# Attention scores of a decoder as plain fp32 products on four groups of 32 partitions, with the maximum as a row of the queries

## The reference, cut to what matters

```python
q = _heads(x @ Wq + bq)                       # (8, 16, 512, 16)
k = _heads(x @ Wk + bk)
v = _heads(x @ Wv + bv)
att = jnp.einsum('bhqd,bhkd->bhqk', q, k) * scale
att = jnp.where(causal[None, None], att, -jnp.inf)
y = jnp.einsum('bhqk,bhkd->bhqd', jax.nn.softmax(att, axis=-1), v)
qc = _heads(x @ Wcq + bcq)
kc = _heads(cross_input @ Wck + bck)          # 1024 context positions
vc = _heads(cross_input @ Wcv + bcv)
attc = jnp.einsum('bhqd,bhkd->bhqk', qc, kc) * scale
y = y + jnp.einsum('bhqk,bhkd->bhqd', jax.nn.softmax(attc, axis=-1), vc)
```

## Time and profile before

| | |
|---|---|
| Median of the runs | 2286.91 us |
| The profiled execution | 2287.69 us, its span 2286.0 us |
| PE (matmul) busy | 2169.5 us, 95% of the span |
| DVE (VectorE) busy | 1366.7 us, 60% |
| ACT (ScalarE) busy | 1102.2 us, 48% |
| POOL (GpSimd) busy | 367.5 us, 16% |
| Mean granted TensorE clock | 0.994 |

### The profile page before, as it was taken

One profiled execution on the slowest core, in us unless ns is written; L12 is line 12 of the kernel. 1 busy time (PEld: TensorE's weight loads), 2 busy tenths in 40 slices (PEclk: granted clock), 3 DMA queues, 4 the chain that ended last, 5 costly groups with the idle time before them and its releaser, 6 DMA issues. The chain is left out here.

```text
span 2286.0 us, 51067 instructions
## 1 busy us (share of the span) xinstructions
PE 2169.5 (95%) x16290; PEld 1352.2 (59%) x16291; DVE 1366.7 (60%) x3905; ACT 1102.2 (48%) x1680; POOL 367.5 (16%) x628
## 2 busy tenths in 40 slices
PE   8999999999899999999999999999999899799998
PEld 4555554556455555555555645554555455499997
DVE  2588357844785458635883478357844685255554
ACT  1267524761477227732674257524762377233332
POOL 1011111111111111111111111111111111122222
PEclk9999999999999999999999999999999999899999
DMA  7440025102520162005300350026102520655553
GB/s 235 155 164 25 2 106 200 48 2 85 198 71 2 47 234 73 2 11 189 130 25 9 141 180 25 1 97 209 48 2 85 198 71 2 221 181 182 183 182 109
DMA packets 115763, 235.75 MB, mean 103 GB/s; under 512 B 19614, under 2 KB 42655, under 8 KB 113344
## 3 DMA queue, kind: packets, MB, share of 16 engines
q1 hardware_dynamic: 112112, 224.23, 29.3%
q0 software_dynamic: 3408, 8.41, 1.0%
HBM read 154.04 MB, written 73.17 MB: 99 GB/s over the span
## 5 line engine op out<-in xcount | busy, mean ns | idle before, releaser
L1201 ACT ACTIVATE es<-ps 128x1024 f32<-128x1024 f32 (+1 forms) x704 | 665.3, 984 | 250.7 <-PE ps L809 181.4
L1412 DVE TENSOR_REDUCE craw<-ps 128x1 f32<-128x512 f32 x1024 | 636.7, 684 | 115.0 <-PE ps L773 115.0
L773 PE MATMUL ps<-hk,hq 64*128 64x512 f32 x1024 | 391.4, 450 | 24.7 <-DVE craw L1412 8.6
L807 PE MATMUL ps<-hq,hk 64*128 64x512 f32 x1024 | 325.0, 440 | 2.2 <-ACT es L1201 2.2
L1408 DVE CUSTOM_DVE_ANT_0 ps<-ps,causal 128x512 f32<-128x512 f32 (+3 forms) x512 | 236.2, 518 | 91.4 <-PE ps L770 91.0
L773 PEld LDWEIGHTS ps<-hk,hq 64*128 64x128 f32 x1024 | 174.7, 184 | 194.8 <-DVE craw L1412 129.3
L809 PE MATMUL ps<-mrow,minus 64*128 64x512 f32 x1024 | 285.8, 391 | 0.0
L837 PE MATMUL ps<-es,vca 128*17 128x256 f32 x4096 | 276.6, 382 | 1.2 <-ACT es L1201 0.3
L661 POOL TENSOR_SCALAR_AFFINE_SELECT es<-es 128x256 f32<-128x256 f32 x256 | 99.0, 406 | 659.5 <-ACT es L1201 659.4
L1731 ACT ACTIVATE hT<-ph,b1s 128x128 f32<-128x128 f32 x312 | 89.2, 369 | 182.8 <-PE ph L1694 182.8
L809 PEld LDWEIGHTS ps<-mrow,minus 64*128 64x128 f32 x1024 | 166.0, 186 | 10.1
(11 more groups left out here) (210 smaller groups left out, 2838.3 us busy)
## 6 DMA issues: line engine op xcount, KB each, us to landing
w1s<-in_w1T SPq DMA_DIRECT2D x39, 1024.0 KB, 5.4
hk<-scr_kc SPq DMA_DIRECT2D x64, 512.0 KB, 5.1
scr_kc<-staged SPq DMA_DIRECT2D x16, 1024.0 KB, 4.3
scr_qc<-staged SPq DMA_DIRECT2D x32, 512.0 KB, 4.5
scr_q<-staged SPq DMA_DIRECT2D x32, 512.0 KB, 5.3
hq<-scr_qc SPq DMA_DIRECT2D x56, 256.0 KB, 4.4
hq<-scr_q SPq DMA_DIRECT2D x56, 256.0 KB, 4.2
hk<-scr_k SPq DMA_DIRECT2D x56, 256.0 KB, 4.6
```

Of the source, the lines that this page charges most:

```text
L773: last = mm(pb, hq[i][at, T + t * P:T + (t + 1) * P], hk[i][at, T + half * BANK:T + (half + 1) * BANK], start=True, stop=True)
L807: mm(pb[a], hk[i][rows[a], T + j * P:T + (j + 1) * P], hq[i][rows[a], T:2 * T], start=True, stop=False)
L1201: nc.scalar.activation(es[:, k % ERING, :].rearrange("p (a c) -> p a c", a=HB)[:, :, 0:w], eslot[k % 2][:].rearrange("p (a c) -> p a c", a ...
L1412: last = v.reduce_max(craw[p % 2][:, t, a:a + 1, 1 + half], pb, AX.X)
```

## The change

- **Products.** The scores are plain fp32 matmuls over 32 partitions. A head's 16 channels lie in every other one of 32 partitions (ROWS), twice: the two heads of a pair have groups 0 and 1 (partitions 0 to 63) for the exponentials and groups 2 and 3 for the maxima. No high and low parts are made.
- **The maximum.** The odd rows of `hk` hold -1, those of `hq` 0. SyncE copies a pair's turned maxima by two DMAs into one odd row of `hq` in groups 0 and 1 (`place_maxima`). The score product then subtracts the maximum itself, and the second matmul is gone. The turned maxima are 16 rows, which ScalarE copies in one instruction in place of four.
- **Staging.** ScalarE or VectorE write each projection once, with its bias, to SBUF (`stage_part`), and SyncE loads a pair's rows from there, each load twice (two DMAs). There are no stores to DRAM and no scratch. There are 4 slots in place of 5, and they are set once by GpSimd (8 memsets before the loop).
- **Order.** One step a cycle: the step k, two maxima (three in the first four steps), then the `weigh` unit of step k-3. After a pair's last `weigh` one cycle goes without, and the next has two and then the turn. Before the steps there are 27 maxima between the parts and 3 behind; the row of a pair goes four maxima behind its last one (two for the first pair).

```diff
-EARLY = 2
-ROW_AFTER = (4, 6)
-BEHIND = 4
-SLOTS = 5
+SLOTS = 4
+LEAD = SLOTS - 1
+MORE_FIRST = 4
+ROW_AFTER = 4
+FIRST_ROW = 2
+BEHIND = 3
 FIRST_PARTS = [("v", 1, 3), ("qc1", 0, 3), ("q1", 0, 3), ("k1", 0, 3),
-               ("qf0", 0, 4), ("qf0", 1, 4), ("qf1", 0, 4), ("qf1", 1, 4)]
+               ("qf0", 0, 4), ("qf0", 1, 4), ("qf1", 0, 4), ("qf1", 1, 3)]
...
-    turns, late = [], []
+    turns, held, kept = [], [], False
     steps = PAIRS * NU
-    for k in range(0, steps + BEHIND, 2):
...
+    for k in range(steps + BEHIND):
+        if k < steps:
+            order.append(("exp", *divmod(k, NU)))
+        order += take(HB + (k < MORE_FIRST))
+        if k >= BEHIND:
+            held.append(k - BEHIND)
+        if kept and k < steps:
+            kept = False
+            continue
+        for m in held:
             order.append(("weigh", *divmod(m, NU)))
             if m % NU == NU - 1:
                 order.append(("keep", m // NU, 0))
+                kept = True
                 turns.append(("turn", m // NU, 0))
...
+        if held and held[0] % NU == 0 and turns:
+            order.append(turns.pop())
+        held = []
...
+            def load(name, p, to, col, done):
+
+                of, first = stage[name], p % (PAIRS // 2) * HB * XD
+                w = of.shape[-1]
+                for u in range(2):
+                    sp.dma_start(to[p % SLOTS][u * HB * ROWS:(u + 1) * HB * ROWS:2, col:col + w],
+                                 of[first:first + HB * XD, p // (PAIRS // 2), :]).then_inc(done[p % SLOTS], 16)
...
+            def place_maxima(b, p):
+
+                sp.wait_ge(s_turned, cur(b, PAIRS, p + 1))
+                sp.sem_inc(s_pace, 1)
+                for a in range(HB):
+                    at = a * ROWS + MAXROW
+                    sp.dma_start(hq[p % SLOTS][at:at + 1, :].rearrange("p (n c) -> p n c", c=P),
+                                 mrow[p % 2][a * 2 * NT:(a + 1) * 2 * NT, :]).then_inc(s_mrow, 16)
...
+            for i in range(SLOTS):
+                nc.gpsimd.memset(hk[i][:], -1.0)
+                nc.gpsimd.memset(hq[i][:], 0.0).then_inc(s_minus, 1)
...
-                pb, at = ring_slot(b, ("max", p, m)), slice(a * HROW, (a + 1) * HROW)
+                pb, first = ring_slot(b, ("max", p, m)), (HB + a) * ROWS
+                at = slice(first, first + ROWS)
...
                 if n == 0:
-                    pe.wait_ge(s_mrow, cur(b, PAIRS, p + 1))
+                    pe.wait_ge(s_mrow, (b * PAIRS + p + 1) * HB * 16)
...
-                    for a in turned:
-                        mm(pb[a], hk[i][rows[a], T + j * P:T + (j + 1) * P], hq[i][rows[a], T:2 * T], start=True, stop=False)
-                    for a in turned:
-                        last = mm(pb[a], neg[a], mrow[p % 2][rows[a], :], start=False, stop=True)
+                rows = [slice(a * ROWS, (a + 1) * ROWS) for a in range(HB)]
+                for j, col in (EXP_SELF[n] if n < NSELF else [(n - NSELF, 0)]):
+                    key, query, w = (j * P, j * P, T - j * P) if n < NSELF else (T + j * P, T, T)
+                    for a in range(HB):
+                        last = mm(pb[a][:, col:col + w], hk[i][rows[a], key:key + P], hq[i][rows[a], query:query + w],
+                                  start=True, stop=True)
...
-                    for t in range(NT):
-                        last = nc.scalar.activation(mrow[p % 2][:, t * P:(t + 1) * P], mbank[n % MBANKS][:, 0:P],
-                                                    ACT.Copy, scale=inblock[:, t:t + 1])
+                    nc.scalar.activation(mrow[p % 2][:], mbank[n % MBANKS][0:MCOLS, 0:P], ACT.Copy).then_inc(s_turned, 1)
```

More of the change, by code:

```diff
@@ L143, in heads_order @@
     order += take(MAXES + AHEAD - sum(count for _, _, count in FIRST_PARTS))
-    turns, late = [], []
+    turns, held, kept = [], [], False
     steps = PAIRS * NU
-    for k in range(0, steps + BEHIND, 2):
[L147 to L150, removed]
-        for m in weighed:
-            if m % NU == 0 and m and order[-1] == ("keep", m // NU - 1, 0):
-                late.append(m)
-                continue
+    for k in range(steps + BEHIND):
[8 more added lines that the diff above has]
+        for m in held:
             order.append(("weigh", *divmod(m, NU)))
@@ L157, in heads_order @@
                 order.append(("keep", m // NU, 0))
+                kept = True
                 turns.append(("turn", m // NU, 0))
-        order += take(1)
-        if k < steps:
-            order.append(("exp", *divmod(k, NU)))
-        order += take(HB)
-        if k + 1 < steps:
-            order.append(("exp", *divmod(k + 1, NU)))
-        order += take(1)
-        order += [("weigh", *divmod(m, NU)) for m in late]
-        late = []
+        if held and held[0] % NU == 0 and turns:
+            order.append(turns.pop())
+        held = []
     assert not maxima
@@ L320, in attentions @@
         x1 = sb("x1", [P, NT, CR])
-        with nc.sbuf_tensor("x1T", [P, KC, T], F32) as x1T:
-            pass
-        hq.append(sb("hq4", [P, 2 * T], F32R))
-        craw = [sb(f"craw{i}", [P, NT, HB, 3]) for i in range(2)]
-        minus = sb("minus", [P, 2], F32R)
-        minus_f = sb("minus_f", [P, 2])
-        inblock = sb("inblock", [P, NT])
+        x1T = sb("x1T", [P, KC, T])
+        craw = [sb(f"craw{i}", [P, NT, HB, 2]) for i in range(2)]
         zk = sb("zk", [P, 2, T // 2])
@@ L566, in _ @@
+            sp.wait_ge(s_minus, SLOTS)
             with sp.Fori(0, nb) as b:
                 following = sp.snap((b + 1) % nb)
-                store(b, "kc0")
                 sp.wait_ge(s_xb, cur(b, 2, 1))
@@ L1140, in _, with stage_part @@
                 nc.scalar.activation(g_s[:, 0, :], t[:], ACT.Copy).then_inc(s_act, 1)
-                def high_part(name, bias_n, m, w, last=True):
-                    stg, at, before = STAGED[name]
-                    t = full(name)
-                    for n in before:
-                        act.wait_ge(s_st[n], cur(b, ST[n], 0 if n in LAST_STAGED else ST[n]))
-                    high = nc.scalar.activation(stage[:, stg, 0, at:at + w], t[:, 0:w], ACT.Identity,
-                                                bias=bias_c[:, bias_n, m:m + 1])
-                    if last:
-                        high.then_inc(s_act, 1)
+                def stage_part(name, bias_n):
+                    m = int(name[-1])
+                    of = stage[name[:-1]]
+                    nc.scalar.activation(of[:, m, :], full(name)[:, 0:of.shape[-1]], ACT.Identity,
+                                         bias=bias_c[:, bias_n, m:m + 1]).then_inc(s_act, 1)
                 t = full("g1")
                 nc.scalar.activation(g_s[:, 1, :], t[:], ACT.Copy).then_inc(s_act, 1)
-                high_part("kc0", 1, 0, TC_)
+                stage_part("kc0", 1)
                 t = full("kv")
@@ L1401, in reduce @@
                     n, a = divmod(m, HB)
+                    if (n, a) == (2 * NT, 0) and p >= 2:
+                        dve.wait_ge(s_ring, cur(b, NRING, RING_AT["row", p - 2, 0] + 1))
+                        dve.sem_inc(s_held, 1)
                     dve.wait_ge(s_ring, cur(b, NRING, s + 1))
```

269 lines of the change are left out of this document (79 added, 190 removed), and 6 rows, old and new, of the table JOBS.

## The result

| | before | after |
|---|---|---|
| Median of the runs | 2287.57 us (4 runs beside it) | 2697.06 us (4 runs, 2678.96 to 2710.71) |
| Ratio | | 1.1785, 95% interval 1.1715 to 1.1855 |
| The profiled execution, its span | 2287.69, 2286.0 us | 2697.38, 2695.7 us |
| Mean granted TensorE clock | 0.994 | 0.977 |
| Period of a sequence without time at half clock | 240.9 us | 285.9 us |

The forecast was 2641 us, range 2480 to 2790. The change costs 409 us.

A forecast was written before the change was run, and what follows sets the result against it. TensorE was taken to set the pace. Heads +37.3, last `weigh` run -0.4, before the steps +8.0 and staging -0.7 gave 44.2 us a sequence, 354 for eight; 2287.7 + 354 - 0.8 gave 2641 us, range 2480 to 2790.

The forecast's parts named there:

- The array's passes: Score products on TensorE: an fp32 pass starts every 0.43 us, four products run abreast, 0.86 us of passes a step.
- The rival by which four groups slow each other: Score products in four row groups: a pass takes 0.56 us instead of 0.43, 0.26 more a step, 2820 us; chance 9%.
- Two passes that hold up the next product: Score products start strictly in program order: five places of 0.43 us, not two, +1.29 a step, 3540 us; chance 3%.
- A step with maxima: Heads: 1.62 us of PE work plus 0.135 of waiting makes 1.755 us a step, 71 steps a sequence, 124.6 us.
- Without maxima: Last 17 steps of a sequence's heads: 1.62 us each for scores and one `weigh` unit, 27.5 us.
- The bank's wait: Three-bank ring: a step's second maximum waits 0.135 us for the bank of the first maximum one step earlier.
- The heads of a sequence: All 88 steps with rows, turns and own units: 165.0 us against 127.7, +37.3; forecast wrong under 150 or over 180.
- Before the steps: Rounds of maxima ahead of the first step: 35.2 us in place of 27.15, +8.0 a sequence, bounds +4 and +11.
- Staging and the row's DMAs at nothing: Projection staging and the maxima row's two DMAs (3.6 us in all) stay hidden; only a 0.68 us wait goes, -0.7.
- The order: Rows of maxima among the steps: seven rows a sequence at 0.6 us each, 4.2 us; the eighth was given nothing.
- The clock: TensorE's granted clock: read at full clock in every slice but one before; no term for half clock in the sum.
- the forecast's 0.11 and 0.1 around the passes: Each step's scores on PE: 0.11 us for first weights, about 0.1 to run out before the array changes shape.

The follow-up runs named there:

- half the reduction: The changed kernel with VectorE reducing only 256 of the 512 columns of each cross unit, leaving half of the cross keys out of its maxima: 2583.95 us, ratio 1.1297.

## Why the prediction was right, and where it missed

- **The array's passes**: right. Passes start 0.43 apart (L734 at 563.12, 563.55 and 563.98), in four groups abreast. The rival by which four groups slow each other is out: 1.07 us for four products, 1.06 for two, and a second pair of products costs 0.96 us in the same groups. The Trainium skill ("TensorE: Matmul & The Clock Gate", Part 3) has 3.07x for row packing of four products. No run here has the four one behind another; by an estimate of 4 x 0.86 and 0.2 around them it would be 3.64 us, 3.4 times the 1.07.
- **Two passes that hold up the next product**: out. The maxima's first passes start at 467.74, ahead of the second passes of the exponentials' products at 468.26, though those products stand ahead in the program. The same Part of the Trainium skill says that matmuls start strictly first in, first out. By products the trace agrees (467.73 and then 467.74); pass by pass, as the rival reads it, it doesn't.
- **A step with maxima**: 1.755 forecast, 1.77 and 1.80 in turn. **Without maxima**: 1.62 forecast, 1.61. **The bank's wait**: 0.135 forecast; 1.785 less the 1.63 to 1.68 with half the reduction is 0.11 to 0.155.
- **The heads of a sequence**: 37.3 more forecast, 38.6 measured where the clock is full (from the first step to the last run of `weigh`, 165.3 in place of 126.8). The parts agree too: a pair with its row, turn and own units is 21.0 us, by the forecast's terms 11 x 1.755 + 0.6 + 1.0 + 0.16 = 21.1.
- **Before the steps**: 35.2 forecast, 34.8 measured, in place of 27.15.
- **Staging and the row's DMAs at nothing**: right. In the heads no wait of PE for a load is in the list of waits of the kernel after, and the idle time of its products that ends with a maximum is 15.8 us for the bank (48 times 0.33) and 8.3 for the last row (8 times 1.04). The wait of 0.68 us for `hq<-staged` is gone, as forecast.
- **The order**: wrong by silence. The sum added up the new heads from seven rows and gave the eighth, that of the last pair, nothing. It has no maxima behind it to hide DVE's last reductions, and the kernel before shows a wait of 1.30 us in that place. It costs 1.1 us a sequence, 9 in all.
- **The clock**: not in the sum. From the last turn of one sequence to that of the next it is 287.4, 303.0, 287.3, 303.4, 285.9, 290.7 and 287.3 us. Only the fifth holds no time at half clock and neither of two waits of PE for `big_b` (1.74 and 1.59 us, in the first two): 285.9 where the forecast has 285.1, 6 us in eight. The falls lengthen the eight sequences by some 46 us, 16 for each of the two long ones, and the two waits add 3. The profiled execution lay 56 us over 2641, and these three are 55 of it. The two sequences with a fall of 34 us take 181 us for the heads, over the 180 that the forecast named as its limit, by the clock alone. With the row moved the kernel takes 2648 us, 7 from the forecast.

So the cause was the forecast's: the plain fp32 form costs 437 us, and the saved second matmul, the staging and the four groups don't pay it back. What the forecast lacked is a term for the clock. It read "at full clock in every slice but one" from the kernel before and priced every step after at full clock; that the total still fell within the range is due to the range's room, not to a bound for the clock.

## What to carry to other kernels

Count the time of passes, not instructions: a plain fp32 product is two passes of 0.43 us, an fp32r product one of half that. Here six fp32r matmuls in two groups (0.64 us of array time) became four fp32 products in four groups (0.86), so even a full array didn't pay for the form. Four row groups do run abreast (1.07 us for four products, 1.06 for two). Each change of shape has its price anew: the forecast's 0.11 and 0.1 around the passes fit the 1.06 us measured. After a change of the products' shape, put the granted clock into the sum as a term with bounds, and look at the end of a written order, where nothing stands behind the last wait.

## What the runs showed of the hardware that was not expected

- The granted clock does not follow from how busy TensorE's records are. PE is busy for 97% of the span after and for 95% before, at a mean clock of 0.977 and 0.994. With the last row moved, maxima in one pass beside exponentials in two have 389 us at half clock, and both in two passes 46. With the row in its place, four groups have 124 and the maxima moved into the exponentials' groups (longer, fewer abreast) 38.
- A fall lasts while the steps go on at half speed, from 3.4 to 34 us in the kernel after and up to 75 us with the maxima in one pass; 34 us cover 11 whole steps. The falls stand at nearly the same places of a sequence, though not in every one.
- A single moved transpose of 0.28 us was worth 49 us of 2697, four fifths of it through the clock. The kernel before waits in the same place for longer and keeps its clock.
